# A planned order for five engines: searching it in eighths, and a second pair of banks for half the first scores

## The reference, cut to what matters

```python
x = x + 0.5 * ffn0(ln(x))    # gate, up, down (704 wide), inputs and weights rounded blockwise to 4 bits
x = x + attn0(ln(x))         # linear attention with decay, sigmoid q and k
x = x + 0.5 * ffn0(ln(x))
x = x + 0.5 * ffn1(ln(x))    # soft mixture: 8 x 128 slots, softmax over the experts and over all slots
x = x + attn1(ln(x))         # 16 heads of 16, causal softmax over 512 tokens, low-rank additions
x = x + 0.5 * ffn1(ln(x))
```

## Time and profile before

| what | value |
|---|---|
| median of three runs | 2616.38 us |
| the profiled execution | 2616.32 us |
| its span, first to last instruction | 2614.5 us |
| PE busy | 2345.9 us, 90% |
| DVE busy | 1920.9 us, 73% |
| ACT busy | 1587.4 us, 61% |
| POOL busy | 871.7 us, 33% |
| mean granted TensorE clock | 0.969 |

### The profile page before, as it was taken

How to read it: one execution, slowest core, us unless ns; L and a number is a source line. 1 busy time by engine, 2 the same in 40 slices (tenths; PEclk the granted TensorE clock), 3 DMA queues, 4 the chain that set the end, 5 groups by cost and what they waited for, 6 DMA issues and landing times.

```text
span 2614.5 us, 54352 instructions
## 1 busy us (share of the span) xinstructions
PE 2345.9 (90%) x22748; PEld 1790.4 (68%) x22748; DVE 1920.9 (73%) x3345; ACT 1587.4 (61%) x2641; POOL 871.7 (33%) x631
## 2 busy tenths in 40 slices
PE   3889888988999998798998999998989999999999
PEld 2556666657677776577776676776766778786787
DVE  8789999999887966767788758677687665545522
ACT  3355546547657573756757584747565577666656
POOL 1122222222322221453626252545435354222022
PEclk9899999999999999899999999998999999999999
DMA  5000000000000000000000000000000000000000
GB/s 174 19 1 1 1 1 1 1 1 1 1 1 1 1 1 25 10 16 4 20 8 20 8 14 14 10 18 14 14 10 20 16 2 10 9 1 9 9 9 9
DMA packets 34979, 33.06 MB, mean 13 GB/s; under 512 B 7664, under 2 KB 34096, under 8 KB 34736
## 3 DMA queue, kind: packets, MB, share of 16 engines
q1 hardware_dynamic: 34736, 29.60, 3.4%
HBM read 12.54 MB, written 4.19 MB: 6 GB/s over the span
## 4 chain that ended last, share of the span: by engine, by line
PE 62%; DVE 23%; ACT 6%; issue 4%; POOL 2%; SPq 1%; DMA 1%; DVEq 0%; ACTq 0%
PE psum L734 16%; PE psum L736 15%; PE psum L735 15%; PE psum L740 5%; PE psum L1161 2%; PE psum L1163 2%; PE psum L1012 2%; PE psum L1162 2%; POOL a1pr L2138 2%; PE psum L1065 2%; DVE a1pr L1900 1%; PE psum L1042 1%; ACT a1PT L1442 1%; DVE a1nm L1877 1%; DVE f1e L2015 1%
## 5 line engine op out<-in xcount | busy, mean ns | idle before, releaser
L2151 POOL TENSOR_TENSOR f1hT<-f1g,f1hT 128x512 f16<-128x512 f32 x256 | 310.4, 1217 | 497.9 <-ACT f1hT L1545 497.3
L2138 POOL TENSOR_TENSOR a1pr<-a1PT,a1pr 128x1024 f16<-128x1024 f32 (+1 forms) x176 | 351.5, 1998 | 338.0 <-DVE a1pr L1900 338.0
L734 PE MATMUL psum<-f1sl,f1w1h 128*128 128x256 f16 x1024 | 283.7, 277 | 12.4 <-ACT f1g L1540 6.4
L734 PE MATMUL psum<-f1w2h,f1hT 128*128 128x256 f16 x1024 | 281.6, 275 | 3.4 <-POOL f1hT L2151 1.3
L735 PE MATMUL psum<-f1sl,f1w1h 128*128 128x256 f16 x1024 | 283.1, 276 | 0.0
L736 PE MATMUL psum<-f1sl,f1w1l 128*128 128x256 f16 x1024 | 282.9, 276 | 0.0
L736 PE MATMUL psum<-f1w2h,f1hT 128*128 128x256 f16 x1024 | 280.9, 274 | 0.0
L735 PE MATMUL psum<-f1w2l,f1hT 128*128 128x256 f16 x1024 | 280.9, 274 | 0.0
L1877 DVE TENSOR_REDUCE a1nm<-psum 128x2 f32<-128x768 f32 (+3 forms) x176 | 198.2, 1126 | 72.4 <-PE psum L992 71.5
L1900 DVE CAST a1pr<-a1PT 128x1024 f16<-128x1024 f32 (+1 forms) x176 | 185.9, 1057 | 83.8 <-ACT a1PT L1442 69.4
L2127 POOL TENSOR_TENSOR f0h<-f0Y,f0sc 128x704 f32<-128x704 f32 x64 | 92.0, 1438 | 386.3 <-DVE f0Y L1746 386.3
(11 more groups left out here) (336 smaller groups left out, 6808.1 us busy)
## 6 DMA issues: line engine op xcount, KB each, us to landing
a1Q<-a1st SPq DMA_DIRECT2D x96, 64.0 KB, 2.6
a1K<-a1st SPq DMA_DIRECT2D x96, 64.0 KB, 2.6
x<-in_L_attn_x SPq DMA_DIRECT2D x8, 512.0 KB, 8.2
out<-x SPq DMA_DIRECT2D x8, 512.0 KB, 3.3
wslot<-in_L_ffn_w SPq DMA_DIRECT2D x1, 1024.0 KB, 8.9
wraw<-in_L_ffn_w SPq DMA_DIRECT2D x1, 1024.0 KB, 5.5
wslot<-in_L_ffn_slot_embeds SPq DMA_DIRECT2D x1, 1024.0 KB, 7.9
a1Q<-a1mr SPq DMA_DIRECT2D x64, 4.0 KB, 1.8
```

The lines of the kernel that those rows point to most:

```text
L734: e.matmul(out, lh, rh, start=start, stop=False)
L2138: e.tensor_tensor(a1["pr"][:, i % 2, 1, :, 0:w], a1["PT"][:, i % 2, :, 0:w], a1["pr"][:, i % 2, 0, :, 0:w], ALU.subtract).then_inc(s["a1_pl"])
L2151: e.tensor_tensor(hT1[:, c % 2, 1, 2 * hp:2 * hp + 2, :], gg[:, hp % 2, :, :], hT1[:, c % 2, 0, 2 * hp:2 * hp + 2, :], ALU.subtract).then_ ...
```

## The change

Two things change. The first is the search over orders. The look-ahead of a play is now one number, 0 or 500 ns, for everything that the play decides itself. The ten plays run with 0. Then, for n = 0 to 7, the first n eighths of the best order so far are kept as they are, and the rest is played anew, twice with 0 and twice with 500 ns, each time with the due times worked out from the play before. Whatever has the earliest modelled end is kept. That is up to 42 plays in place of 10.

The second is the pair of banks of the first scores: in round c = 0 the groups with odd g (5 of 11) write banks 2 and 3 in place of 0 and 1. Round c = 1 and the second scores are as before.

```diff
+def a1_pair(c, g):
+    return 2 if c == 0 and g % 2 else 0
...
-LOOK = 500.0
-LEADS = 1000000.0
+STAGES, TURNS, LOOKS = 8, 2, (0.0, 500.0)
 ROUNDS = 10
...
     late, best = None, None
     for _ in range(ROUNDS):
-        order, end, late = rehearsal(programs, sems, late)
+        order, end, late, done = rehearsal(programs, sems, late, (), 0.0)
         if late is None:
             break
         if best is None or end < best[1]:
-            best = order, end
-    return best
+            best = order, end, late, done
+    for n in range(STAGES):
+        kept = [key for key, _, _ in best[3][:len(best[3]) * n // STAGES]]
+        for look in LOOKS:
+            late = best[2]
+            for _ in range(TURNS):
+                order, end, late, done = rehearsal(programs, sems, late, kept, look)
+                if late is None:
+                    break
+                if end < best[1]:
+                    best = order, end, late, done
+    return best[:2]
...
-        for en in programs:
+        if len(done) < len(kept):
+            en, at, _ = kept[len(done)]
+            best = ((start(en, parts[en][at]), 0.0), en, parts[en][at])
+        for en in programs if best is None else ():
             can = [(t, part) for t, part in ((start(en, part), part) for part in ready[en]) if t is not None]
             if can:
-                first = min(t for t, _ in can)
-                first += LOOK if first > LEADS else 0.0
+                first = min(t for t, _ in can) + look
...
-                        banks.take(0)
-                        banks.take(1)
+                        o = a1_pair(c, g)
+                        banks.take(o)
+                        banks.take(o + 1)
...
-                            sc = [psum[:, odd, i * W:(i + 1) * W] for odd in range(2)]
+                            sc = [psum[:, o + odd, i * W:(i + 1) * W] for odd in range(2)]
...
-                        banks.after(0, "a1_m", (2 * b + c) * NG + g + 1)
-                        banks.after(1, "a1_m", (2 * b + c) * NG + g + 1)
+                        banks.after(o, "a1_m", (2 * b + c) * NG + g + 1)
+                        banks.after(o + 1, "a1_m", (2 * b + c) * NG + g + 1)
...
-                        src = psum[:, 0:2, 0:n * w].rearrange("p o (i k) -> p o i k", i=n)
+                        o_ = a1_pair(c, g)
+                        src = psum[:, o_:o_ + 2, 0:n * w].rearrange("p o (i k) -> p o i k", i=n)
```

More of the change, by code:

```diff
@@ L336, in latest, with rehearsal @@
     return out
-def rehearsal(programs, sems, late):
+def rehearsal(programs, sems, late, kept, look):
     names = {id(v): k for k, v in sems.items()}
@@ L465, in rehearsal @@
     if left:
-        return order, 0.0, None
+        return order, 0.0, None, done
     end = max(clock.values())
-    return order, end, latest(done, end)
+    return order, end, latest(done, end), done
 def perform(program, e, sems, order):
```

## The result

The changed kernel takes 2587.9 us (2586.5 to 2591.2, four runs) against 2616.1 us. The ratio on record is 0.9901, with an interval of 0.9887 to 0.9914, in which the ratio of the two medians, 0.9892, lies too: faster, by 28.2 us between the medians. The forecast was 12 us. The sign and the range (2576 to 2632) held; the size did not, and that is what has to be explained.

The account below looks back on a forecast made before the run. PE was taken as the limit from 600 us and DVE from 200 to 600 us, with the order of work deciding. From 2616.3 us, -3 for the pair and -9 for the search gave 2604 us, range 2576 to 2632.

Parts of the forecast that it names:

- The sum's second term: New search over orders: -9 us, from -7 in the a1 stage and -2 at 200 to 600 us; ends -31 and +9.
- The 2 us of the early stage: From 200 to 600 us, where DVE decides: half of 3.7 us in its fourth slice, taken as -2 us.
- The first term: Second pair of banks for round c = 0: -6 us from alternation, +3 for held bank 3, -3 us in all.
- The mechanism of the held bank: Bank 3 holds a batch's context until scaling, so the next batch's odd groups wait: mean 12.1 us late, priced at 3 us.
- the 45 us: Upper end of held-bank cost in a1's lane: 85 us of lateness over seven batches less 40 us of shorter score runs.
- Rival (a): Held bank decides on PE from 1000 to 2200 us, half the 45 us comes through: slower, 2630 us; chance 0.21.
- The signs that I named: Checks on instruction counts, maxima spacing and order, PE's waits and a1-stage idle (108 to about 98 us), early stage's end, clock.
- Rival (d): Granted clock of the a1 stage falls from 0.96 to 0.92, adding 44 us: 2651 us; chance 0.03.
- Rival (c): Search does more, also trying 500 ns in the first thousand us: all 31 us plus the pair's 3, 2582 us; chance 0.16.
- Rival (b): Nothing comes of it: other waits fill the freed waits on maxima, model's gain stays in the model, 2616 us; chance 0.17.

Follow-up runs that it names:

- old search: Kernel before, with its ten plays and late 500 ns look-ahead, planned anew with the second pair of banks: 2619.4 us, ratio 1.0009.
- four looks: Changed kernel with look-aheads of 150, 250, 350, 500 ns and three turns each per eighth, 106 plays: 2564.5 us; planned with one pair of banks, 2597.0 us.
- three looks: Changed kernel with a third look-ahead of 250 ns added, 58 plays: 2583.0 us; planned with one pair of banks, 2579.5 us.
- run with 500 ns from the start: Kernel before with LEADS = 0, so all ten plays look 500 ns ahead from the first instruction on, one pair of banks: 2644.0 us, ratio 1.0113.
- one-stage search: Changed kernel with one stage in place of eight: ten plays, then two with 0 and two with 500 ns over the whole program: 2586.2 us, ratio 0.9881.

## Why the prediction was wrong in size

**The sum's second term was the error.** The range of 2576 to 2632 held, but that is no merit of the sum, whose centre was 16 us off. The step that failed was: the search "cannot be priced by an instruction", seven slices of the a1 stage brought halfway to the four best, 13.5 us, "I take half: -7 us", with -2 for DVE's slice, -9 in all. Measured, the search with one pair brings 19 us, and 42 plays of the old rule 23; between the two kernels with a second pair (2619.4 and 2587.9) the new search brings 31.5. Two things were missed. The idle time of PE is not the measure of what an order can save: it fell by 14.4 us in the a1 stage (I had said about 10), but 227 more products went through it, which left 24 us less work for the end. I had written that the busy time hides short holes, and then took the sum from it all the same. And I halved the gain a second time, to 7 of 13.5 us, for the model's being no chip, where over these orders model and chip go up and down together with a slope of 0.89.

**The 2 us of the early stage** were not found: DVE was busy for 375.5 us from 200 to 600 against 376.3 us, and at 1000 us PE is 40 products behind.

**The first term, the pair, -3 us with ends of -16.5 and +45, is not settled as a number.** Planned anew with and without it, four comparisons give +3 (old search), -9 (the change), -33 (four looks) and +3.5 us (three looks): a mean of -9 with a scatter as large as that between two orders. What is settled is that its worth isn't a property of the edit. In a given order planned for it, 44 and 49.5 us hang on it; left out before planning, the planner arranges itself with one pair, and nothing is missing in two cases of four.

**The mechanism of the held bank was right in part, and its price was not.** In all seven batches the second maximum comes after the release, as I had said. The delay is smaller: from the first maximum to the second it is now 8.9 us in the mean of the seven, before it was 3.0, so 5.9 us of lateness a batch where I had put 12.1. The planner has moved the context forward: its release now comes 4.2 us after the first maximum in the mean, before 15.9. I had named this way out and given it no price. And the ten maxima that follow take 6.8 us less in these batches, where I had put 5.7. So a round's maxima are done 23.1 us after its first, before 24.0: none of the 45 us is left even in the lane of a1. Rival (a) fails at this place. PE's wait for L1938 in the products with V went from 6.2 to 4.1 us, where I had said it would rise; with all other products that waited for the same scaling it went from 9.8 to 6.2.

**The signs that I named**: equal counts, yes; maxima closer than 1.5 us apart in the first batch, yes for nine of ten steps (the last eight, shown above, start 0.9 to 1.2 us apart); wait for the maxima down to some 10, 6.2; granted clock of the stage 0.95 to 0.97, yes, 0.96 as before. Rival (d) is refuted with that. Rival (c)'s reason, that 500 ns in the first thousand us open something up, is refuted as a rule by the run with 500 ns from the start (2644.0 us). In size (c) came nearest all the same: its 2582 us is 6 us from the measured time, the forecast's 2604 us 16. What it said against itself, that DVE has only 24 us free from 200 to 600 us, did not matter, since the gain was made in the stage of a1. Rival (b) did not happen.

**Open**: why the order of four looks with one pair is 29 us behind its modelled end, and two others, the one-stage search and the 42 plays without eighths, are 19 and 21 us ahead. The gap is as large as the gain under study. The clock doesn't close it: the first of these orders has the clock of the kernel before, and the last, with 0.973 against 0.968 beside it, 4 to 12 us by the two figures above. No run here explains the rest.

## What to carry to other kernels

When the order of a kernel comes from a planner with a model, an edit's time is the edit plus a new draw of the order, and here an order lands some 12 us to either side of its modelled end: compare an edit over several planned orders, or at one order held fixed, and know that the two answer different questions. Try more draws before more cleverness: one number, 10 plays to 42, gave 23 us, and at 42 plays the eighths were 19 us slower than none, a gap that two draws can make. To find where a reordered kernel gained, count the bottleneck's instructions done by a given time; its idle time showed 14 of the 25 us in the stage where the gain was made, and 7 in one where there was none.

## What had not been expected

Finer look-aheads and more plays together did more than anything else tried: with 150, 250, 350 and 500 ns and 106 plays, 2564.5 us, which is 1.96% under the kernel before; no run parts the two. That one order, with its banks, is the best version found. And bank rotation, with groups that stand behind a held bank, cost no clock that can be seen: the granted clock of the profiled executions was 0.969 before, 0.968 after, and 0.970 with the changed order on one pair, and the kernel before alone ranges from 0.963 to 0.972.
